# Other places for the side work of a two-image patch-matching kernel: keys before the ninth-row transfers, patches moved in one group, and a new order at the end

## The reference

```python
embed_w = prelu(conv1x1(x, Wa, ba), aa)
match_in = prelu(conv1x1(x, W1, b1), a1)
raw_w = extract_patches(embed_w, 6, 2)
ref = prelu(conv1x1(mean_2x2(x), W2, b2), a2)           # 24 x 24
w = extract_patches(ref, 3, 1)                          # 576 keys of 144
wn = w / max(norm(w), 1e-4)
yi = softmax(10 * einsum('blc,bqc->blq', wn, patches(match_in)), over the keys)
yd = conv(transposed_conv(yi, raw_w, stride 2), Wd, stride 2) + bd
x1 = x + yd / 6                                         # x in here is gn(x); the residual is the raw x
out = x1 + D @ gn(x1) @ D.T                             # per channel, D the 48 x 48 cosine matrix
```

## Time and profile before

| | |
|---|---|
| times of three runs | 231.97, 232.2, 234.13 us; median 232.2 |
| the profiled execution | 232.2 us, span 230.4 us |
| mean granted clock of PE | 0.881 of full speed |

### The profile page before, as it was taken

The page is one execution under the profiler, slowest core; times in us unless marked ns, Lnnn a source line. Parts: engine busy times, 40 slices in busy tenths (PEclk is TensorE's granted clock), DMA queues, the critical chain, the costliest instruction groups (busy, mean ns, idle before and its releaser), DMA issues.

```text
span 230.4 us, 3498 instructions
## 1 busy us (share of the span) xinstructions
PE 182.9 (79%) x1112; PEld 147.9 (64%) x1112; DVE 142.3 (62%) x293; ACT 118.1 (51%) x209; POOL 122.4 (53%) x107
## 2 busy tenths in 40 slices
PE   1496606963797589396999999999998999698993
PEld 0444506942666478185888878987876776577790
DVE  5669815663576767867566666556778379577101
ACT  4875612657373467545575695565564356133020
POOL 8362101006478489488686599999999940000000
PEclk9996555899679659979999999999999999997687
DMA  5270076666140000243542511440064000004402
GB/s 155 46 129 10 9 138 102 104 116 181 44 77 0 4 0 1 34 81 68 114 126 82 123 32 30 80 81 4 4 127 125 3 3 1 0 0 83 75 3 51
DMA packets 16872, 14.09 MB, mean 61 GB/s; under 512 B 9974, under 2 KB 14646, under 8 KB 16726
## 3 DMA queue, kind: packets, MB, share of 16 engines
q1 hardware_dynamic: 15174, 12.83, 27.7%
q10 hardware_dynamic: 1680, 1.04, 1.6%
HBM read 2.14 MB, written 1.18 MB: 14 GB/s over the span
## 4 chain that ended last, share of the span: by engine, by line
PE 50%; DVE 20%; ACT 9%; POOL 8%; issue 7%; ACTq 3%; DMA 1%; DVEq 0%; SPq 0%; POOLq 0%
PE yt L915 12%; PE ps L873 11%; PE zt L899 9%; POOL nt L692 4%; DVE negm L1392 4%; ACT nt L1105 3%; ACTq L365 3%; PE zt L935 2%; DVE mimg L1338 2%; DVE mhi L1334 2%; PE ps L899 2%; PE yt L950 2%; PE zt L873 2%; ACT slanted L1067 2%; PE pm L943 2%
## 5 line engine op out<-in xcount | busy, mean ns | idle before, releaser
L692 POOL TENSOR_TENSOR nt<-nt 128x599 f32<-128x599 f32 (+1 forms) x51 | 69.2, 1357 | 31.7 <-ACT nt L1113 24.0
L915 PE MATMUL yt<-yf,kf 125*128 125x384 f32 (+1 forms) x120 | 49.6, 497 | 4.8 <-DVE yf L1409 4.7
L899 PEld LDWEIGHTS zt<-ident,nt 128*125 128x125 f32 (+1 forms) x300 | 40.2, 181 | 12.7 <-issue 2.5
L899 PE MATMUL zt<-ident,nt 128*125 128x128 f32 (+1 forms) x300 | 42.4, 279 | 0.1
L1113 ACT ACTIVATE nt<-nt,rps 128x599 f32<-128x599 f32 x36 | 28.7, 796 | 20.0 <-DVE rps L1399 19.9
L1105 ACT ACTIVATE nt<-ps,negm 128x576 f32<-128x576 f32 x31 | 22.9, 738 | 30.3 <-DVE negm L1392 30.3
L1392 DVE TENSOR_REDUCE negm<-ps 128x1 f32<-128x576 f32 x31 | 23.4, 754 | 16.3 <-PE ps L873 15.8
L873 PE MATMUL ps<-wh,vh 128*128 128x288 f32 x62 | 18.5, 383 | 17.6 <-DVE wr L1387 9.1
L873 PEld LDWEIGHTS ps<-wh,vh 128*128 128x128 f32 x62 | 10.7, 214 | 24.1 <-ACT nt L1105 13.8
L915 PEld LDWEIGHTS yt<-yf,kf 125*128 125x128 f32 (+1 forms) x120 | 18.8, 192 | 5.9 <-DVE yf L1409 5.1
L1409 DVE COPY yf<-zt 125x384 f32<-125x384 f32 (+1 forms) x28 | 19.4, 691 | 4.2 <-issue 3.0
(11 more groups left out here) (167 smaller groups left out, 323.6 us busy)
## 6 DMA issues: line engine op xcount, KB each, us to landing
nt<-nt SPq DMA_DIRECT2D x12, 285.2 KB, 3.3
vh<-mimg SPq DMA_DIRECT2D x24, 72.0 KB, 2.5
vl<-mimg SPq DMA_DIRECT2D x24, 72.0 KB, 2.5
emb<-emq SPq DMA_DIRECT2D x32, 18.8 KB, 1.8
v<-x SPq DMA_DIRECT2D x2, 288.0 KB, 4.0
vh<-mimg SPq DMA_DIRECT2D x12, 48.0 KB, 2.2
vl<-mimg SPq DMA_DIRECT2D x12, 48.0 KB, 2.2
x_copy<-v SPq DMA_DIRECT2D x2, 288.0 KB, 2.8
```

Source lines behind the costliest of these rows:

```text
L692: pool.tensor_tensor(nt[:, dst, (to + 1) * KP + 1:(to + 1) * KP + 1 + n], nt[:, one, (row1 + 1) * KP + 1:(row1 + 1) * KP + 1 + n], nt[:, o ...
L899: last = nc.tensor.matmul(turned(sums_bank(m), n, column), keys_at(tile, r + dr, n, shift), ident[:, :], start=at == 0, stop=at == len(wor ...
L915: nc.tensor.matmul(yt[:, k % 2, 0:CHUNK], kf[b][0:n, blk, :], yf[0:n, blk, :], start=blk == 0, stop=blk == KB - 1).then_inc(s_mb, 1)
```

## The change

- `BEFORE`: image 1's `mean`, the second half of the doubling (now a job of its own, `dup`, followed by `after`), and `keys` come before the ninth-row transfers; `weights` of image 1 goes there too.
- `match_patches`: chunk 0 is moved as before; chunks 1 to 5 of image 0 are moved together, one transfer for each of the 8 rows of `vh` and of `vl` (16 in place of 30). `ninth` can do the same: six transfers in place of 18, all ahead of tile 0. All chunks past the first share one count, in `arrived`.
- PE waits for the parts of the keys separately, the high ones before the first pass, the low ones before the second.
- `SPREAD` and `BEHIND_PE` are replaced. For image 1 the slant is a step before DVE's part, `conv1` has a pace of one row a step from step 2 (PE) on, `inorm` and `keys` move from steps 8 to 14 to steps 14 to 16, the embedding's weights are made a step before their use, and `emb` moves from steps 17, 18 to 21, 22.
- The zero rows of `v2` are made by two transfers from zeroed rows of `vr`, at the start, not by POOL's memset.
- `residual` on ACT adds the bias to the first column only; for the others the bias is a scalar of `join_taps`, which is now two instructions per call in place of one.
- At the end the last sums come a step earlier and ahead of the join; `behind` has 3 identities after `zn` of image 0, and image 1's `x1n`, `zn` ahead of image 0's second `d2`, and 2 identities in front of image 1's `d1`, where it had 8, 4 and 2.

```diff
-    ("conv1", 0, (7,)), ("match", 0, (6, 7)), ("ninth", 0, (0, 1, 2)), ("inorm", 0, (0, 1)), ("keys", 0, (0, 1)),
-    ("mean", 1, (0,))]
+    ("conv1", 0, (7,)), ("match", 0, (6, 7)), ("inorm", 0, (0, 1)), ("mean", 1, (0,)), ("dup", 0, (0,)), ("keys", 0, (0, 1)),
+    ("after", 0, (0,)), ("ninth", 0, (0, 1)), ("weights", 1, (0,))]
...
-    ("wst", 0, 1, 0, 1), ("bias_a", 0, 1, 1, 1), ("weights", 1, 1, 1, 1), ("emb", 0, 2, 2, 1), ("ninths", 0, 3, 4, 4),
-    ("bias_2", 1, 1, 4, 1), ("conv2", 1, 2, 5, 1), ("bias_1", 1, 1, 7, 1), ("squares", 1, 1, 8, 1),
-    ("conv1", 1, 8, 9, 3.5), ("match", 1, 8, 11, 3.5),
-    ("norm", 1, 1, 14, 1), ("ek", 0, 2, 28, 2), ("inorm", 1, 2, 25, 3.5), ("keys", 1, 2, 40, 3),
-    ("wst", 1, 1, 46, 1), ("bias_a", 1, 1, 47, 1), ("residual", 0, 1, 33, 1),
-    ("emb", 1, 2, 51, 3), ("ek", 1, 2, 80, 2), ("residual", 1, 1, 66, 1),
+    ("wst", 0, 1, 0, 1), ("bias_2", 1, 1, 0, 1), ("bias_1", 1, 1, 0, 1), ("conv2", 1, 2, 1, 1), ("bias_a", 0, 1, 2, 1),
+    ("emb", 0, 2, 4, 1), ("conv1", 1, 8, 7, 3), ("match", 1, 8, 7, 3), ("squares", 1, 1, 9, 1), ("dup", 1, 1, 29, 1),
+    ("after", 1, 1, 30, 1), ("norm", 1, 1, 20, 1), ("ek", 0, 2, 30, 1), ("residual", 0, 1, 36, 1), ("residual", 1, 1, 37, 1),
+    ("inorm", 1, 2, 42, 3), ("keys", 1, 2, 45, 3), ("wst", 1, 1, 57, 1), ("bias_a", 1, 1, 61, 1), ("emb", 1, 2, 65, 3),
+    ("ek", 1, 2, 85, 3),
...
-    "act": {"conv2": 1, "conv1": 1, "emb": 1, "ek": 1, "zn": 1, "d1": 1, "match": 2},
-    "dve": {"mean": 2, "bias_2": 2, "bias_1": 2, "bias_a": 2, "conv2": 2, "conv1": 2, "emb": 2, "norm": 2,
-            "inorm": 2, "keys": 1, "match": 1, "d1": 2, "d2": 2},
+    "act": {"conv2": 1, "conv1": 1, "emb": 1, "ek": 1, "match": 7, "after": 5},
+    "dve": {"bias_2": 1, "bias_1": 1, "bias_a": 3, "conv2": 3, "conv1": 3, "emb": 3, "norm": 2, "inorm": 2, "keys": 2,
+            "match": 4, "dup": 4},
...
-    behind = stages(1, ("deviation", 1)) + stages(0, ("zn", 3), ("d1", 2))
-    behind += stages(1, ("x1n", 3)) + stages(0, ("d2", 2)) + [("idle", 1, 8)] + stages(1, ("zn", 3)) + [("idle", 1, 4)]
-    behind += stages(1, ("d1", 2)) + [("idle", 1, 2)] + stages(1, ("d2", 2))
+    behind = stages(1, ("deviation", 1)) + stages(0, ("zn", 3)) + [("idle", 1, 3)] + stages(0, ("d1", 2))
+    behind += stages(1, ("x1n", 3)) + [("d2", 0, 0)] + stages(1, ("zn", 3)) + [("d2", 0, 1), ("idle", 1, 2)]
+    behind += stages(1, ("d1", 2), ("d2", 2))
...
+        def arrived(eng, landed, g, images):
+
+            together = 16 * (3 if landed is s_vr else sum(n for _, n in SHIFTS))
+            if images == 1:
+                eng.wait_ge(landed[min(g, 1)], together if g else 48)
+            else:
+                eng.wait_ge(landed[g], (96, together + 48, 48)[min(g, 2)])
...
+                            for row in range(n):
+                                to = F(dst[3 * CR * k + row:3 * CR * k + row + 1, cols])
+                                wide = dst.shape[1]
+                                to = bass.AP(to.tensor, to.offset, [[n * wide, CR], [1, CHUNK * many]])
+                                sp.dma_start(to, bass.AP(src.tensor, at + BLOCK * row,
+                                                         [[pitch, CR], [BLOCK, many], [1, CHUNK]])).then_inc(done, 16)
...
+            for b in range(B):
+                odd = v2[2 * C * b + C:2 * C * (b + 1), :]
+                sp.dma_start(odd, F(vr[128 - C:128, :])).then_inc(s_apart[b], 16)
             ref_patches(0)
-            for t in range(NCH):
-                match_patches(0, t)
+            match_patches(0, 0)
+            match_patches(0, 1, NCH - 1)
...
-                if i == 0 and jb == 0:
-                    pe.wait_ge(s_w[b], 2)
...
+                        arrived(pe, landed, i, b + 1)
+                        if i == 0 and n == 0:
+                            pe.wait_ge(s_whi[b], 3)
+                        if i == 0 and n == 1:
+                            pe.wait_ge(s_w[b], 2)
...
-                nc.scalar.activation(v2[part, :], v2[part, :], ACT.Identity, bias=bd6[part, 0:1]).then_inc(s_xres[b], 1)
+                first = strided(x1(b), 0, (W, H))
+                nc.scalar.activation(first, first, ACT.Identity, bias=bd6[x1_rows(b), 0:1]).then_inc(s_xres[b], 1)
...
+                if k == NG - 3 and j == 2:
+                    last_sum(0)
+                if k == NG - 2 and j < 2:
+                    last_sum(j + 1)
+                if k == NG - 2 and j == 2:
+                    last_pair(NG - 1)
                 if k >= 1 and j == 2 and (k - 1) % NCH in (2, 4, 5):
                     b, part = (k - 1) // NCH, ((k - 1) % NCH - 1) // 2
                     join_taps(b, part)
```

More of the change, by code:

```diff
@@ L360, in strided, with ninth @@
             return bass.AP(ap.tensor, ap.offset + start, [list(ap.ap[0])] + [list(d) for d in dims])
[L362 to L366, removed]
+        def ninth(eng, n, low, t, many=1):
+            src = F(mimg[64 + low:64 + low + CR, :])
+            at = src.offset + match_rows_at(1 + SHIFTS[2][0], t + 2, 0)
+            return eng.dma_start(F(vr[CR * n:CR * (n + 1), CHUNK * t:CHUNK * (t + many)]),
+                                 bass.AP(src.tensor, at, [[mimg.shape[1], CR], [BLOCK, many], [1, CHUNK]]))
+        def arrived(eng, landed, g, images):
[4 more added lines that the diff above has]
+                eng.wait_ge(landed[g], (96, together + 48, 48)[min(g, 2)])
         def patches_in(eng, images):
-            for g in range(NCH):
-                for landed in (s_vh[g], s_vl[g], s_vr[g]):
-                    eng.wait_ge(landed, 48 * images)
+            for g in range(NCH if images > 1 else 2):
+                for landed in (s_vh, s_vl, s_vr):
+                    arrived(eng, landed, g, images)
         def place_free(eng):
@@ L738, in deviation @@
                 inverse_root(mv2[rows, :], mhalf[rows, :], s_var2[b], s_root2[b])
-            handlers = {"xs": pooled, "mean": mean, "squares": squares, "norm": inverse_norms, "residual": odd_taps, "deviation": deviation}
+            handlers = {"xs": pooled, "mean": mean, "squares": squares, "norm": inverse_norms, "deviation": deviation}
             zeros()
@@ L1026, in match_high @@
                         after(b, 1)
-                        after(b, 2)
                     return
@@ L1051, in ninth_taps @@
                 for n, low in enumerate((0, CR, 0)):
-                    ninth(nc.scalar, n, low, t).then_inc(s_vr[t], 16)
+                    ninth(nc.scalar, n, low, t, NCH - 1 if t else 1).then_inc(s_vr[t], 16)
             def residual(b, _):
@@ L1154, in cosine_w @@
                 nc.scalar.activation(d1[:, CHUNK * i:CHUNK * (i + 1)], o[0:2 * H, 0:CHUNK], ACT.Copy).then_inc(s_free["act"], 1)
-            handlers = {"match": match_high, "ninth": ninth_taps, "ninths": lambda b, i: ninth_taps(b, 3 + i), "residual": residual, "conv2": lambda b, i: slant("conv2", b, i, 96, 1),
+            handlers = {"match": match_high, "after": lambda b, i: after(b, 2), "ninth": ninth_taps, "residual": residual, "conv2": lambda b, i: slant("conv2", b, i, 96, 1),
                         "conv1": lambda b, i: slant("conv1", b, i, 96, 0),
@@ L1446, in join_taps @@
             def join_taps(b, part):
-                first, n = CLASSES[2 * part], 2
-                dims = (W * NCH, ROWS), (W, n), (1, W - 1)
-                even = strided(x1(b), W * first + 1, *dims)
-                odd = strided(v2[2 * C * b + C:2 * C * (b + 1), :], W * first, *dims)
-                nc.vector.tensor_tensor(even, even, odd, ALU.add).then_inc(s_x1[b], 1)
-                dve.wait_ge(s_x1[b], part + 1)
+                for n in range(2):
+                    t = CLASSES[2 * part + n]
+                    dims = (W * NCH, ROWS), (1, W - 1)
+                    even = strided(x1(b), W * t + 1, *dims)
+                    odd = strided(v2[2 * C * b + C:2 * C * (b + 1), :], W * t, *dims)
+                    nc.vector.scalar_tensor_tensor(out=even, in0=even, scalar=bd6[x1_rows(b), 0:1], in1=odd, op0=ALU.add,
+                                                   op1=ALU.add).then_inc(s_x1[b], 1)
+                    dve.wait_ge(s_x1[b], 2 * part + n + 1)
             def x1_statistics(b, i):
```

53 lines of the change are left out of this document (26 added, 27 removed).

## The result

| | kernel before | changed kernel |
|---|---|---|
| median, timed side by side | 232.69 us (231.97 to 234.13) | **237.4 us** (236.05 to 238.72) |
| ratio | | 1.020, 95% interval 1.014 to 1.026 |
| profiled execution | 232.2 us, span 230.4 | 238.72 us, span 236.9 |
| mean granted clock | 0.881 | 0.868 |

A forecast was written before the change was run, and what follows sets the result against it. It saw a front waiting for keys, a stalled fill, POOL bounding the sums from 132.60, and a late tail. Gains 6.0 + 7.2 + 0.8 - 0.2 + 3.5 = 17.3 off span 230.4, plus 1.8 around it, gave 215 us, range 208 to 226.

The forecast's parts named there:

- Keys first: At the front: PE's score 0 ends about 35.4, some 3.3 us sooner, with keys ahead of the ninth-row issues.
- Grouped patches: Before tile 3: transfers at 165 GB/s (bounds 100 and 195), low parts at about 45.5, exp 3 at about 49.
- Rival D: Grouped transfers don't overlap, the last low part lands at 66 and PE waits at tile 3: 235.5 us, chance 0.07.
- The fill: From exp 3 to exp 11: a DVE step of 3.05 us brings exp 11 at 75.3, gain 6.0 us.
- Rival A: DVE and patches hold the fill back, with a step of 3.6 and low patches at 49: 222 us, chance 0.22.
- Tiles 11 to 17: Six tiles at 3.49 plus 2.1 us make 23 instead of 30.2, gain 7.2 us; bounds 20.9 and 27.
- score 18: Just after tile 17: waits for DVE's low part of image 1's later keys, priced at 1.3 us (0 to 3).
- Tiles 17 to 35: Up to the end of POOL's row sums: memset saves 2.1 us, score 18 costs 1.3, gain 0.8 us.
- DVE's end: DVE's work between its first and last pair, with the join as two instructions: loss 0.2 us, bounds 0 and 0.99.
- The tail: After the last pair: image 1's transpositions start sooner in the new order, gain 3.5 us (1 to 5).
- The bias pass: ACT's 2.20 us pass over 32x2304, listed among the stalls whose removal gives tiles 11 to 17 their 7.2 us.
- rival E: New PE stalls at tiles 12 to 18 and a fallen tail clock: 229 to 231 us, chance 0.1 together with another rival.

The follow-up runs named there:

- Experiment 4: The kernel before with only the keys and image 1's mean moved ahead of the ninth-row issues; 231.5 us, ratio 0.990.
- experiment 1: The changed kernel with chunks 1 to 5 of the query patches moved and waited for one by one, ninth rows still grouped; 226.6 us, ratio 0.973.
- experiment 2: The changed kernel with the join as one addition of 32x752, the bias of columns 1 to 47 left out; 231.2 us, ratio 0.990.
- experiment 3: The changed kernel with the order and identities at the end as before (8, 4 and 2); 239.0 us, spread too wide for a ratio.
- Experiment 12: The changed kernel with only 8, 4 and 4 identities in the reordered tail; 234.6 us, ratio 1.003.
- Experiment 10: experiment 7 with image 1's doubling, four casts, moved from DVE to ACT; 225.3 us, ratio 0.975.
- experiment 7: experiment 5 with the bias back as a ScalarE pass over the whole raw image, at steps 12 and 22; 224.0 us, ratio 0.961.
- experiment 5: The changed kernel with chunks issued one by one and the join as one addition, bias of columns 1 to 47 left out; 223.5 us, ratio 0.957.
- experiment 9: experiment 7 with 8, 4 and 4 identities in the reordered tail where it had 3, none and 2; 220.6 us, ratio 0.949.
- experiment 11: experiment 7 with the added tail identities and image 1's doubling on ACT together; 225.4 us, four runs between 219.4 and 228.2.

## Why the prediction was wrong, by its own steps

1. **Keys first: right.** Score 0's last pass is at 33.99, forecast 35, and exp 0 at 35.67 (39.59 before). Experiment 4 shows this term nearly alone.
2. **Grouped patches: the step that failed, 6.5 of 23.8 us.** "I take 165, nearer to the upper, since the present flow does not queue." In the forecast's own terms, 2.36 MB from 31 us on, the last low part at 52.0 makes 112 GB/s (an estimate), not 165: near the lower bound of 100, which would give 54.6. All transfers together moved 138 GB/s, with the engines busy for 0.88. The upper bound was leaned on for lack of a row that shows what a full queue gives. The windows of before would have shown that the flow called free of queues already held the engines busy for 0.66 of the time from 31 to 53.6 us, at 121 GB/s; in proportion a full share would be 183 GB/s for all transfers together (an estimate), and 138 was reached. A second fault lay in the structure, not in the figure: the forecast put the wait of tile 3 for the last patch at the front's 3.3 us and did not ask what the same kernel would do with chunks. There lay 10.8 us (experiment 1). Rival D put its finger on the same wait, but its mechanism, transfers that do not overlap, did not come: an issue leaves every 1.09 us and lands 5 us later, so four to five are in flight. It decided only from a landing at 63; it was 52.
3. **The fill: right, the match to 0.1 us by luck.** Exp 3 to 11 in 26.4, forecast 26.3. Within it errors cancel: exp 3 to 5 took 6.8 us, forecast 8, and a step behind it 3.27, forecast 3.05. The profiles of experiments 2, 3 and 12, where this stretch is the same code, have 24.6. The split's mean is 0.64 us, forecast 0.89. The subtraction's 0.76, forecast 0.68, is over both images; image 1's eight take 0.97 on the mean. Rival A's dearer step of 3.6 did not come.
4. **Tiles 11 to 17: mis-sized, 6.0 us.** The forecast took six steady tiles and 2.1. But PE alone is busy 23.44 of the 28.99 us, at a granted clock of 0.88; 23 would have needed a PE without a hole through the densest side work. By tile, exp 11 to 12 took 7.3 us, 12 to 13 5.2, 13 to 14 4.5 and 16 to 17 5.3, against the 3.49 of a steady one; before, 11 to 12 took 4.0. Experiment 10 takes 3.2 us off 11 to 12 by moving the doubling to ACT, but only 1.3 off the whole stretch. How the other 4 to 5 divide between the keys (DVE's small low key of 16x288 took 1.43 us), score 18 and the clock was not taken apart. Score 18's last wait was 0.95 us, and exp 18 came 4.6 behind exp 17: within the bounds given.
5. **Tiles 17 to 35: the join, and POOL as the bound, 8.3 us.** "I take 0.2" for a second instruction, under "DVE's end". It was looked for on DVE behind the last sum, where it costs little. But there are three more joins within the steady part, ahead of a maximum, and each cost 1.4 to 2.2 us more. 6.6 of the 8.3 went with one instruction for two (experiment 2). The prediction had the rule on the ports and used it for splits only. The other 1.7 us are in a second fault: "the end of the row sums is POOL's from 132.60 on", so that the memset's 2.1 us were counted as won. The earlier trace rows has PE busy for 30.46 of 31 us in the same window, more than POOL's 29.31. Without the memset and with the joins as before, exp 18 to 35 took 59.75 us, before 59.73 (experiment 2): the memset was worth nothing there, with the side work where the change has it. Exp 17 to 18 took 1.5 us more than before (forecast 1.3). In the changed kernel POOL's last sum ended 11.2 us behind exp 35's start, 12.55 before; it did not end this stretch there either.
6. **DVE's end: near.** PE's hole is 1.51 us, 2.35 before, and the last turned group starts 23.2 us behind exp 35 (23.7 before): 0.5 won where 0.2 was to be lost.
7. **The tail: the order right, the clock not, 3.0 us.** Bounds of 1 to 5 were given, "1 if the clock then falls". It fell: 0.63, then 0.50, and the tail from the last value product on got 0.6 us shorter (24.4 before, 23.8 after). Experiment 12 puts 4 us on the clock.
8. **The bias pass: overrated.** It stands among the stalls of tiles 11 to 17; experiment 7 has it back in both images for 0.5 us.

In time rival D came nearest (235.5), by luck, as its mechanism was another; in mechanism rival E did (229 to 231, new stalls and a fallen clock), with too low a chance. Neither had the join. With three of the four errors taken back one behind the other (experiments 1, 5 and 9, and 7 for the bias), the change's other parts give 220.6 us. They don't simply add: the join is worth 6.2 us alone and 3.1 behind experiment 1. By the marks, that kernel's profile is 5.9 us over the forecast: exp 11 comes at 73.8, 1.5 ahead of it, 11 to 17 takes 29.3, 6.3 over, 17 to 35 65.0, 2.3 over, and the rest 50.9, 1.2 under. So the error of point 4 is the one that stays.

## What to carry to other kernels

When many transfers become few, ask first which piece the consumer needs first; where the DMA engines were already busy for two thirds of the time, as here, larger transfers brought the last byte only 1.7 us forward, and one count over all of them makes the first consumer wait for it. Count an instruction that is split at each place where it runs, not at the last one, and price each piece at up to a whole instruction of the engine that it takes turns with. Before work is taken off an engine for a gain, look whether a second engine is just as busy in the same stretch: POOL lost 2.2 us here, and PE did not let them through. A reordered tail is to be priced together with the clock that it will run at: four microseconds hung on eleven more identity products, and they did not hold the clock in each execution.

## What was not expected of the hardware

- Row pieces from SBUF to SBUF: 30 transfers of 48 and 72 KB and 16 of 120 KB had their last byte there 1.7 us apart. In the same stretch of 21.6 us the DMA share was 0.68 at 113 GB/s (chunk by chunk) and 0.88 at 138 GB/s (grouped), and an issue on SP's queue grew from 0.62 to 1.09 us.
- DVE and POOL took turns instruction by instruction: 1.25 became 1.77 or 2.15 us on POOL, 0.55 became 1.7 on DVE, and one join 0.93 or 2.00, depending on which was first by 0.03 to 0.2 us.
- The tail's clock stood at 1.00 for 13 us in experiment 9, and fell from about 206 us in one execution of experiment 11 with the same fillers and the same order. What decides between the two is open.
